# Multi-query attentions: two chunks of probabilities transposed in a row, then two attends

## The reference, cut to what matters

```
q = (xn @ Wq) -> 16 heads of 64        k, v = xn @ Wkv (one head of 64), null key and value put in front
sim = q k^T + bias[h]                  causal, masked
out = softmax(sim) v                   then @ Wo and a layer norm
```

## Time and profile before

| | us |
|---|---|
| median of 3 runs | 5019.03 |
| lowest and highest run | 4993.03, 5105.1 |
| the profiled execution: its own time, as span from first to last instruction | 5025.5 |
| TensorE matmuls busy | 4231.0 (84%) |
| TensorE weight loads busy | 2953.0 (59%) |
| VectorE busy | 2608.1 (52%) |
| ScalarE busy | 1893.5 (38%) |
| GpSimd busy | 197.9 (4%) |

### The profile page before, as it was taken

The page is one execution under the profiler, slowest core; times in us unless marked ns, Lnnn a source line. Parts: engine busy times, 40 slices in busy tenths (PEclk is TensorE's granted clock), DMA queues, the critical chain, the costliest instruction groups (busy, mean ns, idle before and its releaser), DMA issues. The chain is left out here.

```text
span 5025.5 us, 72372 instructions
## 1 busy us (share of the span) xinstructions
PE 4231.0 (84%) x24072; PEld 2953.0 (59%) x24074; DVE 2608.1 (52%) x6227; ACT 1893.5 (38%) x4293; POOL 197.9 (4%) x611
## 2 busy tenths in 40 slices
PE   8989999968888983457888888768889886999999
PEld 5555655645555561344555555645555565888888
DVE  4544355456566638545555555346665644443443
ACT  1124455425555512213555554125555531222221
POOL 0000000000000000000000000000000000000000
PEclk8988598969999995657999999879998997999999
DMA  1000000011111100000000000011111201000000
GB/s 33 16 9 4 1 4 2 5 51 63 54 50 66 39 9 17 8 15 9 10 18 10 9 10 17 4 52 40 62 54 42 68 15 34 18 18 34 18 18 17
DMA packets 84997, 128.69 MB, mean 26 GB/s; under 512 B 11772, under 2 KB 58884, under 8 KB 84759
## 3 DMA queue, kind: packets, MB, share of 16 engines
q1 hardware_dynamic: 84758, 125.53, 7.7%
HBM read 123.33 MB, written 2.17 MB: 25 GB/s over the span
## 5 line engine op out<-in xcount | busy, mean ns | idle before, releaser
L689 ACT ACTIVATE cond_p<-cond_p,cond_negm 128x128 f32<-128x128 f32 (+7 forms) x768 | 592.0, 772 | 291.6 <-DVE cond_negm L727 288.3
L653 PE MATMUL ps_s<-cond_k_high,cond_q_high 65*128 65x512 f32 (+3 forms) x1152 | 492.3, 429 | 248.8 <-DVE cond_q_both L56 207.0
L626 PE MATMUL ps_o<-cond_pt,cond_v 128*64 128x256 f32 (+1 forms) x3840 | 619.6, 403 | 17.8 <-DVE attn_out L759 17.8
L664 PE MATMUL ps_t<-ident,cond_p 128*128 128x128 f32 x3456 | 592.6, 293 | 0.7 <-ACT cond_pt L695 0.7
L695 ACT COPY cond_pt<-ps_t 128x512 f32<-128x512 f32 x576 | 314.3, 546 | 656.2 <-PE ps_t L664 651.7
L664 PEld LDWEIGHTS ps_t<-ident,cond_p 128*128 128x128 f32 x3456 | 417.7, 147 | 175.4 <-issue 123.3
L727 DVE CUSTOM_DVE_ANT_0 cond_p<-ps_s,cond_side,cond_null_score 128x128 f32<-128x128 f32 (+7 forms) x512 | 413.3, 817 | 193.4 <-PE ps_s L653 182.5
L653 PEld LDWEIGHTS ps_s<-cond_k_high,cond_q_high 65*128 65x128 f32 x1152 | 228.1, 198 | 458.0 <-DVE cond_q_both L56 277.5
L653 PE MATMUL ps_s<-cond_k_both,cond_q_both 128*128 128x512 f32 (+3 forms) x1152 | 408.1, 366 | 0.0
L2023 ACT ACTIVATE moe_hid<-ps_s,moe_b 128x512 f32<-128x512 f32 x256 | 176.1, 688 | 496.3 <-PE ps_s L1986 496.3
L727 DVE CUSTOM_DVE_ANT_0 attn_p<-ps_s,attn_causal 128x128 f32<-128x128 f32 (+7 forms) x272 | 202.3, 757 | 239.3 <-PE ps_s L653 237.8
(11 more groups left out here) (315 smaller groups left out, 7353.2 us busy)
## 6 DMA issues: line engine op xcount, KB each, us to landing
cond_side<-in_fside_16xSxS SPq DMA_DIRECT2D x32, 512.0 KB, 6.0
moe_w<-in_L_ffn_W SPq DMA_DIRECT2D x16, 1024.0 KB, 7.3
cond_side<-in_fside_16xSxS SPq DMA_DIRECT2D x32, 448.0 KB, 5.1
cond_side<-in_fside_16xSxS SPq DMA_DIRECT2D x32, 384.0 KB, 4.6
cond_side<-in_fside_16xSxS SPq DMA_DIRECT2D x32, 320.0 KB, 4.2
cond_side<-in_fside_16xSxS SPq DMA_DIRECT2D x32, 256.0 KB, 3.4
cond_toep<-distance_bias SPq DMA_DIRECT2D x16, 512.0 KB, 4.3
cond_side<-in_fside_16xSxS SPq DMA_DIRECT2D x32, 192.0 KB, 3.2
```

The costliest lines, as they stand in the source:

```text
L626: last = nc.tensor.matmul(m.O[n % 2][h * W:(h + 1) * W, s0 * P:PH * P], a.values(h, b, kb), PT[c % PTS][:, (h * PH + s0) * P:(h + 1) * PH ...
L653: last = nc.tensor.matmul(bank(it, n, EX + r)[:, lo:hi], x, y, start=(i == 0), stop=(i == len(parts) - 1))
L664: last = nc.tensor.transpose(m.T[c % 2][:, r * P:(r + 1) * P], Pr[n % 2][r][:, kb * P:(kb + 1) * P], m.ident[:, :])
L689: nc.scalar.activation(p, p, ACT.Exp, bias=negm[n % 2][:, r:r + 1], scale=-1.0, accum_out=rsum[n % 2][:, r:r + 1]).then_inc(exped, 1)
```

## The change

`plan` takes two chunks in one step where `ahead` is set (`together` = 2) and one where it is not. The rows that fall into either of the two chunks come first, then both transpositions, then the attends until only `LAG` chunks are left behind, which is two attends, and then the exponentials of all rows of the step. `den`, `halves`, and whatever `ends` holds for either chunk come after that. The number of instructions of every kind is the same, and so are LAG, buffers and banks.

```diff
         placed = 0
-        for kb in range(blocks):
+        together = 2 if ahead else 1
+        for kb in range(0, blocks, together):
             late = []
-            while placed < len(rows) and placed * span < (kb + 1) * len(rows):
+            while placed < len(rows) and placed * span < (kb + together) * len(rows):
                 steps.append(("row", n + 1, rows[placed]))
                 late.append(("exp", n + 1, rows[placed]))
                 placed += 1
-            steps.append(("chunk", n, kb, chunk))
-            lagging.append((n, kb, chunk))
-            if len(lagging) > LAG:
+            for i in range(together):
+                steps.append(("chunk", n, kb + i, chunk + i))
+                lagging.append((n, kb + i, chunk + i))
+            while len(lagging) > LAG:
                 steps.append(("attend",) + lagging.pop(0))
             steps += late
             if kb == 0:
@@ -459,8 +461,9 @@
             if halves is not None:
                 steps.append(halves)
                 halves = None
-            steps += ends.pop(chunk, [])
-            chunk += 1
+            for i in range(together):
+                steps += ends.pop(chunk, [])
+                chunk += 1
```

## The result

| | before | after |
|---|---|---|
| median, us | 5008.28 (4 runs, 4993.03 to 5105.1) | 5306.5 (4 runs, 5266.19 to 5394.41) |
| profiled execution, span | 5025.5 | 5264.4 |
| granted clock, whole span | 0.880 | 0.855 |
| the three loops, from first matmul to last | 720.8 + 788.4 + 724.0 = 2233.2 | 818.1 + 878.7 + 819.6 = 2516.4 |

After takes 1.058 times the time of before, 95% interval 1.044 to 1.072. It is slower, as forecast (5268 us, range 5160 to 5360). Some runs of each of these kernels are 1.5% or more longer than its fastest, at a lower granted clock, and ratios and intervals leave them out, while medians hold all runs.

What follows compares the result with a forecast made beforehand. TensorE's program order was taken to bound the attention loops. Four-chunk units +137, six-chunk +38, eight-chunk +5 gave +180 us; the clock +69 made +249 on the 5019 median: 5268 us, range 5160 to 5360.

Steps and rivals of the forecast that it cites:

- The mechanism: Four-chunk unit: four exponentials ahead of `fin` on ScalarE delay the first attend 3.87 us; net 3.05, 45 times, +137 us.
- What would show it: Signs: four-chunk first attend waits about 3.6 us, some 160 in all; four exponentials in a row; double groups; lower clock.
- The joins: TensorE's transpositions and attends: joining two groups saves 0.30 us a pair, 0.25 behind a row, at most 144 us.
- The six-chunk unit: Lost cover of the second row less joins +0.3 us, late copy +0.5; together 48 x 0.8 = +38 us.
- The eight-chunk unit: Second row loses 1.2 us of cover, four pairs save 1.1; 48 x 0.1 = +5 us.
- The clock: Half-clock spells of 1.5 us behind two thirds of four-chunk and one third of eight-chunk idle stretches: 46 spells, +69 us.
- the two bounds: Limits on the slow-clock cost: no spells, 0, or a spell behind all 93 stretches at 1.5 us, 140 us.
- the wait doesn't grow: Rival: four-chunk wait for `attn_out` stays as it was because ScalarE is further ahead; 5079 us, chance 0.10.
- only TensorE's order counts: Rival: joined groups pay in full, -144 us, and waits hide behind the time won; 4875 us, chance 0.05.
- The clock falls behind every new gap: Rival: slow clock after every new idle stretch in four- and eight-chunk units, 180 + 140 = +320; 5339 us, chance 0.15.
- Joins save nothing: Rival: weights are not loaded ahead on TensorE, so 113 us come on top; 5381 us, chance 0.04.
- The two-chunk unit: Its rows come first in either order, so it only gains its joined groups: -0.30 us.

Runs made afterwards that it cites:

- Two pairs of kernels that differ in nothing else: TensorE's transpositions and attends in turns instead of joined: against the changed kernel, 5449.71 us; against the version with one row ahead and later `attn_out`, 5047.44 us.
- The experiment that only filled one wait: Changed kernel plus eight useless 512-column matmuls on TensorE ahead of the four-chunk unit's wait for `out`: 5224.89 us, ratio 1.039 to the kernel before.
- the fastest version: Changed kernel with one row ahead of a unit's first pair, others behind their pair, `fin` and `out` two units later: 4888.43 us, ratio 0.971 to before.

## Why the prediction was right, and what it mis-sized

- **The mechanism**: `fin` behind four exponentials holds the first attend. Right in place, cause and size: 9.62 us from second row to attend (9.80 forecast), 45 times as counted, and from the second row to the next projection 1371.84 - 1361.21 = 10.63 against 7.47 before, +3.16 at full clock (3.35 forecast). The kernel before with only this changed loses 120 us; moving two exponentials out of the way gives back 155.
- **What would show it**: "the first attend waits about 3.6 us, some 160 us in all". 3.42 at full clock (the terms of the prediction give 3.7, 9.80 less 6.1, not 3.6), but 107.6 in all: at half clock TensorE comes late to the wait and the idle time is spent as slow work instead. The sum of idle time understates what a wait costs when the clock falls too. The other signs came as said: four exponentials in a row, double groups of 1.04 and 1.08 us, and a clock of 0.84, 0.88 and 0.83 in the loops, where before has 0.93, 0.93 and 0.92.
- **The joins**: forecast 144 us at most, 0.30 or 0.25 a pair. Two pairs of kernels that differ in nothing else give 132 and 125 us in the loops, and 0.30 and 0.33 a pair in eight-chunk units. Weights of the next matmul are loaded during the running one although all of them use the same 128 rows: eight joined transpositions take 0.96 us (1331.50 to 1332.46, where the attends behind them start), and they start every 0.109 us, though the load of one takes 0.14. The reading from rows 3 and 5 was right. The sentence of the Trainium skill ("TensorE: Matmul & The Clock Gate", The mechanism) that ties such an overlap to different row groups does not hold for these matmuls; the same section also allows it for a background weight buffer, which fits.
- **The six-chunk unit**: forecast +0.3 for cover and joins and +0.5 for the late copy. The late copy is there ([0.39 <-DVE cond_pt] at 1333.94). From the second row to the next projection 1335.76 - 1326.37 = 9.39 us against 11.88 - (1382.74 - 1379.58) = 8.72 before: +0.67. Ahead of the second row it is 4.11 against 3.16, and that is the clock: the projection, 1.51 us from its start to the first row (1322.26 to 1323.77) against 0.78 at full clock (1335.76 to 1336.54), runs in the spell behind the `attn_out` wait. Units that ran wholly at full clock agree: +0.60 (12.48 against 11.88).
- **The eight-chunk unit**: +0.1 forecast, -0.08 measured. Its second row does wait longer (1.86 against 0.81) as forecast.
- **The clock, the mis-sized term**: +69 us forecast as 46 spells of 1.5 us. Without it the parts, measured at full clock, come to 3.16 - 0.30 + 0.67 - 0.08 = 3.45 us a set of four units; over some 46 sets 159 us, of 283. The rest, about 124 us, is what is left for the clock, 55 more than forecast and near the upper of the two bounds, 140. (By the right-hand columns of the table, with 7.58 for the two-chunk unit, a set costs 3.11 us and the clock 140.) The experiment that only filled one wait took back 86 us. The price of a spell was right: 1.48 us in before, as said. Their number and place were not. Counted from the granted clock in the traces, the loops of before have 57 stretches at half clock with 311.5 us in all, those of after 128 with 748.9: 71 more, not 46, of 5.9 us on average against 5.5. A third of the new ones was to fall behind the eight-chunk wait, where the clock mostly stayed at 1.00 (window 1338.90 to 1349.00; 24 of 30 such units in the `cond2` loops); they come behind waits that stood there before, too, of the two-chunk unit (1.69 us) and of the four-chunk unit's second row (1.31 against 0.95 before). In the set shown that makes three stretches with 17 us at half clock, against 3.4. That a gap brings slower work behind it was right (in after the clock is 0.67 to 0.70 in the stretches behind each of the three waits), and the Trainium skill ("TensorE: Matmul & The Clock Gate", HAM oscillation) agrees in direction; no row ahead of the prediction let me count the gaps that do.
- **The total**: +283 in the loops against +249; the medians of the runs differ by 298. The forecast of 5268 came within 0.8% of the measured median, inside its range. That it came so near is luck in part: the work at full clock was put 21 us too high (180 against 159) and the clock 55 too low.
- **Rivals**: "the wait doesn't grow" (5079) and "only TensorE's order counts" (4875) fall with the 3.42 us wait. "The clock falls behind every new gap" (5339) is a little nearer to 5306.5 than the forecast (33 against 39 us), but wrong in place, as just told. "Joins save nothing" (5381) falls with the two comparisons.

Open: why the same wait of 1.69 us is followed by half clock at one time and by full clock at another. After has half clock behind it (stretch from 1299.70) and the kernel with the filled wait full clock (second row at 1308.42, clock 1.00 to 1315.40). The order of the work does not decide it, since the kernel before shows both with one and the same list. Of its 32 two-chunk units in the `cond2` loops 7 ran wholly at full clock, as the second of these, a set behind the first:

```profile
1359.67:1369.04 9.37, 7.23 (x32) 4.23 (x31) 5.19 (x17) 3.05 (x9) 0.40 (x1) 0.82 0.00 0
1403.70:1411.58 7.88, 5.75 (x33) 3.60 (x32) 5.19 (x17) 1.78 (x5) 0.82 (x3) 1.00 0.02 6
```

The wait in the second of them:

```profile
1406.86 0.50 PE L653 MATMUL ps_s<-cond_k_high,cond_q_high 65*128 65x512 f32 x1 [1.68 <-DVE cond_q_both L56]
```

What does decide, no run here shows. The two-chunk unit's +0.48 instead of -0.30 is the clock: in the `cond2` loops these units run at a mean clock of about 0.80 in before and 0.70 in after, and at full clock the new order gives the -0.30 that was forecast (7.58 against 7.88).

## What to carry to other kernels

Where one list of steps orders several engines, regrouping for the busiest one regroups the queues of the others: look for the short instruction that ends up behind a batch of long ones (here a copy of 0.36 us behind four exponentials) and for who waits on it. Moving that instruction alone passes the lateness to the next in the queue; spreading the batch kept 42 us of the gain, with an interval that includes none. Spreading it further and giving the waiting result two units of time, both at once, made this kernel 2.9% faster, all of it by the joined groups; which of the two keeps their gain was not tested. Price an idle stretch of TensorE at more than its length, since the work behind it may run at half clock, and compare versions by the time between fixed steps of the program rather than by summed idle time.

## What the runs showed of the hardware

- Useless matmuls can pay: eight of 512 columns in a wait of 3.4 us, 42 times, made the loops 86 us shorter and raised the granted clock of the first loop from 0.84 to 0.93. In the `cond1` loop they changed neither (0.88, 3 us).
- At half clock TensorE's work takes twice as long, start to start: 0.109 and 0.213 us from one transposition to the next, 0.216 and 0.427 for the matmuls of a projection, 0.78 and 1.51 from a projection's start to the next row's. The kernel loses less than that, since waits on the other engines, which keep their speed, shrink meanwhile (3.42 to 2.02 us): the loops of after have 437 us more at half clock than those of before (748.9 and 311.5), and the estimate above leaves 124 to 140 us for it, about 0.3 us for each.
- What a pair of joined groups saves depends on what TensorE waits for beside it: 0.30 and 0.33 us in eight-chunk units, 0.10 in six-chunk units and nothing in two-chunk units at full clock of the fastest version.
- The same wait of 1.69 us in the same order of work is followed by half clock in most sets of before and by full clock in some: 9.36 and 7.88 us for the unit.
